# One scatter more per tile in the message pass, one less beside the first convolution

## The chip, the cores and the metric

One Trainium2 chip; the kernel runs on 1 of its cores. The metric is the device time in microseconds of one execution. The kernel before takes 4446.39 us, the median of three timed runs (4443.1 to 4448.91).

## The reference

A graph network of four layers on 6250 nodes with 96 features and 100000 edges that are sorted by destination. After each layer the result is added to x and normalised over the features.

```python
dst = (6250 * uniform(100000) ** 2).astype(int)       # then sorted; src is uniform
# layer 0: softmax aggregation
m = relu(x[src]) + 1e-7
a = exp(m - seg_max(m, dst)[dst]); a = a / seg_sum(a, dst)[dst]
x = norm(x + (x + seg_sum(a * m, dst)) @ W + b)
# layer 1: messages
msg = mlp(concat([x[src], x[dst], mlp(edge_attr)]))
x = norm(x + seg_sum(msg, dst) + mlp(x))
# layers 2 and 3: two mean convolutions each
conv(h) = (seg_sum(h[src], dst) / max(deg, 1)) @ Wl.T + b + h @ Wr.T
x = norm(x + conv(relu(conv(x)))); x = norm(x + conv(elu(conv(x))))
```

## The kernel before, in words

**Two edge passes.** The edges are padded and cut into 196 tiles of 512 (4 columns of 128 edges). The softmax pass and the message pass each go over the 196 tiles, with a ring of 4 tiles in the buffers. For each tile POOL issues four indirect DMAs that gather the source rows (L770, one for 128 edges). In the message pass SP loads two tiles at a time (L590 to L627): attributes, keys, flags, ranks, and eight windows of 128 rows of the destination table (L626, 48 KB each). PE sums the message in PSUM (L935, L941, L942; it waits for the gathers and windows), ACT applies relu and takes sums (L1230, L1234), DVE scans over the edges (L1682), PE turns the result back (L953), and ACT stores it.

**The adjacency matrix.** The four convolutions multiply with a matrix in DRAM, `adj`, of 51 x 51 blocks of 128 x 128 float16 counts. The softmax pass clears it. Each edge writes its count into one cell. During the message pass DVE computes for each tile the counts of its four columns (`count_copies`, L1643) and the cells (`redirect`, L1655). POOL writes them with indirect DMAs of 128 elements of two bytes, one for each column. The scatters in the pass go through the columns in order, NOW of them for each tile, three tiles behind: tile t issues columns NOW x (t - 3) and the next. So the first EARLY = 196 x NOW columns of the edge list are written in the pass, beside the gathers, in `gather_and_scatter` (L790, with the scatter at L781). Within it POOL takes the gathers in NOW portions and puts a scatter behind each; before the first scatter it waits for DVE's `redirected`. DVE's `redirect` waits until the scatters of the tile four before have landed.

**The late scatters.** The remaining columns, up to 782, are written by POOL after the pass (L855 to L862). Before them POOL gathers the ends of the runs for the node stage (L836, 49 of them). They go in batches of 8; after each batch POOL waits for the batch before it and raises `adj_ready` (L846 to L849).

**The first convolution.** PE first projects the nodes in 13 packs of four node tiles (L1072 transposes, L1083 matmuls, with DVE's `split_pack`, L1831, and ACT between). Then come 49 jobs, one for each node tile: 49 matmuls of 128 x 288 each (L1111) on a stripe of `adj`, 1568 KB, which SP loads into one of four slots (`fill_first`, L662). SP waits for `adj_ready` until the batches are in that hold the edges of the node tile; how many it needs is worked out on DVE from the degrees (`tile_ready`, L1522 to L1526). As the edges are sorted by destination, the job of node tile j needs all columns up to its last edge. Between and behind the jobs there are two joint jobs (L1120, of 49 matmuls; their stripes at L673, which wait for `ROWS_DONE` batches), then one load of 3136 KB of links (L680, once 48 jobs are summed), and the link matmuls (L1138) with the packs of the second convolution. The three other convolutions have 51 jobs each (L1181) and end the kernel.

Of the kernel before, what the change touches and what calls it, by code (L numbers as in the profile page):

```python
# [17 lines left out]
P = 128  # L18
F = 96
CH = 4  # L20
# [12 lines left out]
SLOTS = 4  # L33
PACK = 4
REPEAT = 1024
NOW = 2
BATCH = 8

MATRICES = ["W0", "W_node", "W_src", "W_dst", "W_ef"]
# [8 lines left out]
def joints(n_edges):  # L48

    return math.ceil(edge_tiles(n_edges) / P)  # L50
# [28 lines left out]
def build(nc, n_edges, x_in, chunk_last_in, node_rows_in, dst_cols_in, dst_before_in, dst_seq_in, src_cols_in, node_cols_in, next_row_in,  # L79
# [20 lines left out]
    EXT = joints(n_edges)  # L100
# [5 lines left out]
    SCATTERS = math.ceil(n_edges / P)  # L106
    EARLY = ET * NOW
    LATE = CN - EARLY
    BATCHES = math.ceil((SCATTERS - EARLY) / BATCH)
    assert LATE > 0 and SCATTERS > EARLY  # L110
    FIRST_ROUNDS = 7
    ROWS_DONE = [1 + math.ceil((min((i + 1) * P * CH, SCATTERS) - EARLY) / BATCH) for i in range(EXT)]
    assert ROWS_DONE[-1] == BATCHES + 1

    ctx = ExitStack()
    with ctx:
        def sb(name, shape, t=f32):
            return ctx.enter_context(nc.sbuf_tensor(name, shape, t))

        def dram(name, shape, t=f32):  # L120
            return nc.dram_tensor(name, shape, t, kind="Internal").ap()
# [18 lines left out]
        CELLS = JOBS * P * KB * P  # L140
        adj_all = dram("adj", [CELLS + (RING * NOW + LATE) * P, 1], f16)
        adj = adj_all[0:CELLS, :].rearrange("(t p c) a -> t p (c a)", p=P, c=KB * P)
# [125 lines left out]
        copies = tail(P, CN)  # L268
        cell_ring, is_repeat = sb("cell_ring", [P, RING, NOW], i32), sb("is_repeat", [P, RING, NOW], i32)
        copies_ring = sb("copies_ring", [P, RING, NOW], f16)  # L270
        elsewhere_late = cells(P, LATE).bitcast(i32)
# [7 lines left out]
        one_h = sb("one_h", [P, 1], f16)  # L279
        elsewhere = sb("elsewhere", [P, RING, NOW], i32)  # L280
        weigh = sb("weigh", [P, TE + (CH - 1) * P], bf16)
# [258 lines left out]
        def _(sp):  # L540
# [130 lines left out]
            def fill_joint(i):  # L671
                sp.wait_ge(adj_ready, ROWS_DONE[i])
                sp.dma_start(joint_slots[:, i, :, :].rearrange("p b n -> p (b n)"), adj[NT + i, :, 0:NT * P])\  # L673
                  .then_inc(joint_landed, 16)
# [33 lines left out]
        def _(pool):  # L708
# [3 lines left out]
            def iota(t, pattern, step):  # L712
                return nc.gpsimd.iota(t, pattern=pattern, base=0, channel_multiplier=step,
                                      allow_small_or_imprecise_dtypes=True)
# [30 lines left out]
            iota(iota_p[:, :], [[0, 1]], 1)  # L745
            nc.gpsimd.iota(elsewhere[:, :, :], pattern=[[P * NOW, RING], [P, NOW]], base=CELLS, channel_multiplier=1)
            nc.gpsimd.iota(joint_row[:, :], pattern=[[1, ET]], base=NP, channel_multiplier=0,
# [1246 lines left out]
```

How the kernel before makes its waits and increments, by code:

```python
def wait(eng, semaphore, value):  # L61
    if not (isinstance(value, int) and value <= 0):
        eng.wait_ge(semaphore, value)
# [8 lines left out]
    def do(self, instruction):  # L73
        self.n += 1
        instruction.then_inc(self.semaphore, 1)
        self.eng.wait_ge(self.semaphore, self.base + self.n)
# [446 lines left out]
        def wait_for_tables(eng, p):  # L523
            if PASSES[p] == MESSAGE:
                eng.wait_ge(node[p - 1]["stored"], 16 * NG)
                eng.wait_ge(node[p - 1]["dst_stored"], 16 * NT)
# [11 lines left out]
        @block.sync  # L539
        def _(sp):
            sp.dma_start(chunk_last, chunk_last_in).then_inc(lasts_landed, 16)
            sp.dma_start(attr_f, attr_in.rearrange("(p j) -> p j", p=P)).then_inc(attr_in_landed, 16)
            sp.dma_start(x_sb[:, 0:FULL, :], x_in[0:FULL * P, :].rearrange("(k p) f -> p k f", p=P)).then_inc(x_landed, 16)
            sp.wait_ge(consts_made, 1)
            sp.dma_start(x_sb[0:REST, FULL, :], x_in[FULL * P:n_nodes, :]).then_inc(x_landed, 16)
            sp.dma_start(w_edge[:, :], w_edge_in).then_inc(attr_in_landed, 16)
            sp.dma_start(seq_now, dst_seq_in[1:1 + EP].rearrange("(p j) -> p j", p=P)).then_inc(seq_landed, 16)
# [4 lines left out]
            sp.dma_start(src_cols, src_cols_in).then_inc(idx_landed, 16)  # L552
            sp.wait_ge(relu_made, 1)
            sp.dma_start(relu_table.rearrange("(k p) f -> p k f", p=P), hidden[:, 0:NT * F].rearrange(
# [72 lines left out]
                if kind == SOFT:
                    sp.wait_ge(zeros_made, 1)
                for h in range(RING // 2):
```

## Time and profile before

| | |
|---|---|
| Median of the timed runs | 4446.39 us |
| Span of the profiled execution, the only time that is given of it | 5171.8 us |
| PE busy | 3159.9 us (61%), 18737 matmuls |
| DVE busy | 2679.3 us (52%) |
| POOL busy | 2510.8 us (49%) |
| ACT busy | 1560.3 us (30%) |
| DMA | 387596 packets, 797.88 MB |
| Softmax pass, first to last gather | 84.2 to 1243.8 us |
| Message pass, first gather to last scatter | 1453.5 to 3186.7 us |
| Late scatters, first to last | 3268.4 to 3787.8 us |
| First link matmul | 4112.5 us |

All times in the rows are of that one profiled execution, counted from its first instruction. An engine's busy time leaves out register, branch and semaphore instructions and the issue of DMAs on SP and ACT; POOL's indirect DMAs are counted as busy. "issue" stands where an engine waited for nothing that the profile shows, "remote" where the release came from something that the profile doesn't name. SPq is SP's queue.

### The profile page before, as it was taken

Reading aid. Unit: us, or ns where it says so; the run is one execution under the profiler, and the core shown is the slowest. Engines: PE = TensorE matmul, PEld = TensorE weight load, DVE = VectorE, ACT = ScalarE, POOL = GpSimd, SP = SyncE. Lnnn points to the kernel's source line nnn. Section 1 sums busy time; section 2 is a strip of 40 time slices with the busy share of each in tenths; the row PEclk is TensorE's granted clock in tenths of the full one; section 3 lists DMA queues with packets and bytes.
Section 4 is the critical chain, followed back from the end, with each engine's and each line's share of the span. In section 5 each row is a group of like instructions: output and inputs, shape, how many; then the busy total and the mean of one; then the engine's idle time right before and its main releaser. Section 6 shows DMA issues by size and latency. Waiting matters only on the chain.

```text
span 5171.8 us, 61853 instructions
## 1 busy us (share of the span) xinstructions
PE 3159.9 (61%) x18737; PEld 2317.1 (45%) x18737; DVE 2679.3 (52%) x5868; ACT 1560.3 (30%) x3684; POOL 2510.8 (49%) x2587
## 2 busy tenths in 40 slices
PE   1555555554755555555555554111159999999999
PEld 0333333333534344344344333100047777788777
DVE  4888888888645555555555556300001254433333
ACT  1777777776222222222222222100000011111000
POOL 7666666664666666666666666777720000000000
PEclk9999999999986667667667666555579999999999
DMA  5555555555134444444444443100037666666776
GB/s 183 192 198 191 195 194 194 192 192 164 56 98 111 112 121 111 116 117 111 114 118 112 111 118 85 58 0 0 13 126 282 215 218 245 247 248 251 259 276 228
DMA packets 387596, 797.88 MB, mean 154 GB/s; under 512 B 207412, under 2 KB 264600, under 8 KB 361128
## 3 DMA queue, kind: packets, MB, share of 16 engines
q1 hardware_dynamic: 239330, 586.35, 33.9%
q0 software_dynamic: 82320, 90.28, 7.9%
q10 hardware_dynamic: 65718, 118.62, 6.2%
q8 instruction: 93, 1.52, 0.1%
q14 instruction: 135, 1.11, 0.1%
HBM read 581.03 MB, written 213.92 MB: 154 GB/s over the span
## 4 chain that ended last, share of the span: by engine, by line
PE 25%; issue 23%; SPq 19%; DVE 3%; another core or an unknown queue 1%; DMA 0%; ACTq 0%; ACT 0%; DVEq 0%; POOL 0%
PE ps L1181 18%; SPq L626 14%; PE ps L1111 6%; SPq L601 1%; SPq L596 1%; SPq L622 1%; SPq L607 1%; SPq L617 1%; PE ps L1064 1%; ACTq L64 0%; DMA area<-adj 0%; PE ps L1083 0%; PE ps L1056 0%; DVE second L1650 0%
## 5 line engine op out<-in xcount | busy, mean ns | idle before, releaser
L770 POOL DMA_INDIRECT area<-src_table,early x784 | 752.5, 960 | 469.6 <-remote 225.5
L770 POOL DMA_INDIRECT area<-relu_table,early x784 | 739.6, 943 | 421.3 <-issue 212.4
L953 PE MATMUL ps<-ident,area 96*128 96x96 f32 x2352 | 441.4, 356 | 804.3 <-issue 555.4
L953 PEld LDWEIGHTS ps<-ident,area 96*128 96x128 f32 x2352 | 355.2, 213 | 939.2 <-issue 782.4
L1181 PE MATMUL ps<-second,area 128*128 128x288 bf16 x5194 | 652.1, 286 | 0.2 <-DVE second L1823 0.2
L1682 DVE TENSOR_TENSOR_SCAN area<-flags,area,ps 96x512 f32<-96x512 int8 x196 | 250.0, 1276 | 647.6 <-issue 552.0
L1181 PEld LDWEIGHTS ps<-second,area 128*128 128x128 f16 x5194 | 509.0, 98 | 128.5 <-DVE second L1823 0.5
L1650 DVE SCALAR_TENSOR_TENSOR second<-second,area,ps 128x512 bf16<-128x512 f32 x784 | 538.1, 741 | 0.0
L857 POOL DMA_INDIRECT adj<-out_ring x390 | 395.5, 1014 | 127.8 <-issue 127.8
L781 POOL DMA_INDIRECT adj<-copies_ring,cell_ring x392 | 388.6, 991 | 125.6 <-issue 118.9
L1111 PE MATMUL ps<-early,area 128*128 128x288 bf16 x2401 | 322.0, 292 | 204.9 <-issue 204.9
L1230 ACT ACTIVATE ps<-ps,msg_bias 96x512 f32<-96x512 f32 x196 | 126.7, 647 | 1042.5 <-remote 911.0
L942 PE MATMUL ps<-second,area 128*96 128x128 f32 x1568 | 378.1, 328 | 34.1 <-issue 33.8
L941 PE MATMUL ps<-ident,area 128*96 128x128 f32 x1568 | 382.4, 334 | 7.8 <-issue 7.1
L941 PEld LDWEIGHTS ps<-ident,area 128*96 128x96 f32 x1568 | 301.0, 215 | 170.3 <-issue 170.2
L925 PE MATMUL ps<-ident,area 128*96 128x128 f32 x784 | 208.0, 421 | 265.8 <-DVE second L1705 184.9
L1111 PEld LDWEIGHTS ps<-early,area 128*128 128x128 f16 x2401 | 236.7, 99 | 290.0 <-issue 231.7
L916 PE MATMUL ps<-attr,w_edge_parts 36*96 36x512 bf16 x392 | 235.3, 601 | 185.2 <-DMA attr<-attr_parts 118.7
L1695 DVE TENSOR_TENSOR_SCAN second<-ps,second 96x512 f32<-96x512 f32 x196 | 249.5, 1273 | 159.7 <-remote 153.7
L1181 PE MATMUL ps<-early,area 128*128 128x288 bf16 x2597 | 331.8, 286 | 0.0
L935 PE MATMUL ps<-second,w_ef_scaled 96*96 96x512 f32 x392 | 306.6, 875 | 0.4 <-issue 0.4
L942 PEld LDWEIGHTS ps<-second,area 128*96 128x96 f32 x1568 | 283.8, 210 | 23.5 <-issue 23.4
(330 smaller groups left out, 4709.0 us busy)
## 6 DMA issues: line engine op xcount, KB each, us to landing
area<-adj SPq DMA_DIRECT2D x147, 1632.0 KB
area<-adj SPq DMA_DIRECT2D x55, 1568.0 KB
adj<-early SPq DMA_DIRECT2D x102, 816.0 KB
soft_sums<-out_ring ACTq DMA_DIRECT2D x196, 384.0 KB
second<-key_dram SPq DMA_DIRECT2D x98, 512.0 KB
area<-dst_table SPq DMA_DIRECT2D x784, 48.0 KB
sums<-out_ring ACTq DMA_DIRECT2D x196, 192.0 KB
second<-caps_dram SPq DMA_DIRECT2D x98, 192.0 KB
```

Source lines behind the costliest of these rows:

```text
L626: sp.dma_start(dst_rows[:, s + c // CH, c % CH, :], dst_table[bass.ds(firsts[c], P), :])\
L770: pool.indirect_dma_start(out=src_rows[:, s, c, :], out_offset=None, in_=gather_table[p], in_offset=bass.IndirectOffsetOnAxis(ap=src_cols[ ...
L781: pool.indirect_dma_start(out=adj_all, out_offset=bass.IndirectOffsetOnAxis(ap=cell_ring[:, s, c:c + 1], axis=0), in_=copies_ring[:, s, c: ...
L857: pool.indirect_dma_start(out=adj_all, out_offset=bass.IndirectOffsetOnAxis(ap=cell_late[:, c:c + 1], axis=0), in_=copies_late[:, c:c + 1] ...
L935: nc.tensor.matmul(bank(s % 2, F), w_ef_scaled[:, :], h_ring[:, s % 2, :], start=True, stop=False)
L941: nc.tensor.matmul(ps[0:F, s % 2, at], src_rows[:, s, c, :], ident[:, :], start=False, stop=False)
L942: last = nc.tensor.matmul(ps[0:F, s % 2, at], dst_rows[:, s, c, :], rank_hot[:, s % 2, at], start=False, stop=c == CH - 1)
L953: last = nc.tensor.transpose(ps[:, b, c * F:(c + 1) * F], r[:, (s * CH + c) * P:(s * CH + c + 1) * P], ident[0:F, 0:F])
L1111: last = nc.tensor.matmul(bank(lane % 2, P, PARTS_F), slots[:, lane, s, :], y[:, s, :, :].rearrange("p c f -> p (c f)"), start=s == 0, sto ...
L1181: last = nc.tensor.matmul(bank(b, P, PARTS_F), slots[:, lane, s, :], y[:, s, :, :].rearrange("p c f -> p (c f)"), start=s == 0, stop=s == ...
L1650: last = v.scalar_tensor_tensor(same[:, c, :], keys[:, s, :], key[:, bass.ds(t * CH + c, 1)].bitcast(f32), around, ALU.is_equal, ALU.mult, ...
L1682: v.tensor_tensor_scan(out=slot(sum_ring, s), data0=flags[:, s, :], data1=bank(s % 2, F), initial=last_of(sum_ring, s), op0=ALU.mult, op1= ...
```

## The change

NOW goes from 2 to 3: three scatters for each tile are issued in the message pass. EARLY, LATE, BATCHES, `tile_ready` and the rings that are NOW columns wide follow from it. With 588 early columns the first joint stripe (columns up to 512) needs no late batch, so the count for it is held at zero.

```diff
-NOW = 2
+NOW = 3
...
-    ROWS_DONE = [1 + math.ceil((min((i + 1) * P * CH, SCATTERS) - EARLY) / BATCH) for i in range(EXT)]
+    ROWS_DONE = [1 + math.ceil(max(min((i + 1) * P * CH, SCATTERS) - EARLY, 0) / BATCH) for i in range(EXT)]
```

In `gather_and_scatter` a tile's order on POOL changes from two gathers, scatter, two gathers, scatter to gather, scatter, gather, scatter, two gathers, scatter.

## Rows read from the trace of the kernel before

**Rows 1.** The page, part 4: the chain that ended last, by engine and line

```profile
PE 25%; issue 23%; SPq 19%; DVE 3%; another core or an unknown queue 1%; DMA 0%; ACTq 0%; ACT 0%; DVEq 0%; POOL 0%
PE ps L1181 18%; SPq L626 14%; PE ps L1111 6%; SPq L601 1%; SPq L596 1%; SPq L622 1%; SPq L607 1%; SPq L617 1%; PE ps L1064 1%; ACTq L64 0%; DMA area<-adj 0%; PE ps L1083 0%; PE ps L1056 0%; DVE second L1650 0%
```

**Rows 2.** Waits, 1900 to 3100 us: total us, times, longest us

```profile
POOL area L770 <- remote: 164.9, 62, 2.9
```

**Rows 3.** Timeline of POOL, two tiles: start us, us, [idle before]

```profile
2510.86 0.97 POOL L770 DMA_INDIRECT area<-src_table,early  x1 [2.52 <-remote]
...
2513.38 0.99 POOL L781 DMA_INDIRECT adj<-copies_ring,cell_ring  x1 [0.30 <-issue]
2514.68 0.96 POOL L770 DMA_INDIRECT area<-src_table,early  x1 [0.30 <-issue]
...
2528.39 0.97 POOL L770 DMA_INDIRECT area<-src_table,early  x1 [2.54 <-remote]
```

**Rows 4.** Windows: us, busy and count by engine, granted clock, DMA share, GB/s

```profile
1900.00:2500.00 600.00, 344.07 (x1566) 240.80 (x1567) 343.30 (x959) 168.10 (x409) 396.52 (x410) 0.69 0.44 115
```

**Rows 5.** Line L626, 1456.15 to 1458.2 us: ns min/median/max, first and last start

```profile
L626 SPq DMA_DIRECT2D area<-dst_table x4: 167/346/411, 1456.2 to 1457.8; - x4
```

**Rows 6.** Timeline of SP: the window loads of two tiles, later

```profile
2515.14 13.29 SPq L626 DMA_DIRECT2D area<-dst_table  x8
```

**Rows 7.** Timeline of PE: packs, then matmuls of early jobs

```profile
3283.72 1.47 PE L1083 MATMUL ps<-w_conv,hidden 97*128 97x192 f32 x8
...
3290.86 1.57 PE L1083 MATMUL ps<-w_conv,hidden 97*128 97x192 f32 x8 [1.99 <-issue]
...
3345.58 1.06 PE L1072 MATMUL ps<-ident,x_sb 128*96 128x128 f32 x4
...
3379.17 1.06 PE L1072 MATMUL ps<-ident,x_sb 128*96 128x128 f32 x4
...
3794.48 0.40 PE L1111 MATMUL ps<-early,area 128*128 128x288 bf16 x1 [2.40 <-issue]
3797.28 0.40 PE L1111 MATMUL ps<-early,area 128*128 128x288 bf16 x1 [2.40 <-issue]
...
3816.18 4.03 PE L1111 MATMUL ps<-early,area 128*128 128x288 bf16 x18 [0.28 <-issue]
```

**Rows 8.** Timeline of POOL: the late scatters, early and at their end

```profile
3283.03 0.97 POOL L857 DMA_INDIRECT adj<-out_ring  x1 [0.30 <-issue]
...
3787.76 1.09 POOL L857 DMA_INDIRECT adj<-out_ring  x1 [0.30 <-issue]
```

**Rows 9.** Lines L770, L781 and L857, whole trace, as in rows 5

```profile
L770 POOL DMA_INDIRECT area<-relu_table,early x784: 938/944/957, 84.2 to 1243.8; - x196
L770 POOL DMA_INDIRECT area<-src_table,early x784: 947/955/980, 1453.5 to 3171.7; - x196
L781 POOL DMA_INDIRECT adj<-copies_ring,cell_ring x392: 963/991/1005, 1471.1 to 3186.7; - x196
L857 POOL DMA_INDIRECT adj<-out_ring x390: 962/967/1907, 3268.4 to 3787.8; - x195
```

**Rows 10.** Timeline of DVE: the running maximum of two tiles

```profile
697.00 1.28 DVE L1695 TENSOR_TENSOR_SCAN second<-ps,second 96x512 f32<-96x512 f32 x1 [2.09 <-remote]
702.05 1.28 DVE L1695 TENSOR_TENSOR_SCAN second<-ps,second 96x512 f32<-96x512 f32 x1
```

**Rows 11.** DMA issues: KB each, median us to landing

```profile
second<-adj SPq DMA_DIRECT2D x2, 1568.0 KB, 9.7
area<-adj SPq DMA_DIRECT2D x1, 3136.0 KB, 14.1
```

**Rows 12.** Line L1138, as in rows 5

```profile
L1138 PE MATMUL ps<-early,area x294: 206/206/281, 4112.5 to 4153.9; 128*128 128x96 bf16 x147
```

**Rows 13.** Groups by line, 3820 to 4096 us: count | busy us, mean ns | idle

```profile
L1111 PE MATMUL ps<-early,area 128*128 128x288 bf16 x2206 | 270.6, 286 | 0.0
```

**Rows 14.** Groups by line, 1900 to 3100 us, DVE, as in rows 13

```profile
L1661 DVE TENSOR_SCALAR is_repeat<-area 128x2 int32<-128x2 f32 x136 | 26.0, 191 | 4.7
```

## The prediction

> **What bounds the kernel now.** I read the page's chain first [rows 1]. It names SP's window loads (L626) with 14% and gives 23% to "issue", time in which an engine waited for nothing that the profile shows. Taken as it stands, it says that SP paces the message pass. So I went to that pass. In the stretch from 1900 to 3100 us POOL waits 62 times for 2.7 us, once in two tiles [rows 2]. Its timeline shows the pattern [rows 3]: 12 indirect DMAs for two tiles, a gather every 1.26 us and a scatter every 1.30 us from start to start, then a pause; two tiles take 17.53 us, of which POOL needs 8 x 1.26 + 4 x 1.30 = 15.3 us, or 7.64 us a tile. PE and DVE are busy for 5.0 us a tile and ACT for 2.5 (POOL's count over its six a tile, 410 / 6 = 68 tiles in 600 us) [rows 4]. Only SP and POOL come near the pace.
>
> Then I asked whether SP's pace is real. At the start of the pass four window loads are issued 0.53 us apart [rows 5]; later eight of the same size take 13.29 us, 1.66 us each [rows 6]. PE shows the same in the first convolution: four-tile packs follow each other every 3.6 us at first (two in the 7.14 us shown) and every 33.6 us afterwards, and the matmuls of the first jobs stand 2.80 us apart, with no semaphore to blame [rows 7]. A pack is 12 matmuls and 12 weight loads, so 48 starts and ends: 0.70 us each. A job's matmul with its weight load has 4: 0.70 us again. POOL's late scatters go from 1.27 to 1.40 us at the end, each with its idle time before it, which is 2 x 0.70 [rows 8]. One start or end in 0.70 us, on three engines, whatever the work: I read this as the recording of the trace holding the engines, which a timed run doesn't have. That is an inference, and the sum tests it, since the span of 5171.8 us is 725 us above the median of 4446.39.
>
> **The time rebuilt without that.** First gather at 84 us [rows 9]. Softmax pass: 196 tiles at 5.05 us, the distance of two maxima without a wait [rows 10], 990. From its last gather (1243.8) to the message pass's first (1453.5), 210, taken as it is [rows 9]. Message pass: 196 x 7.64 = 1497. The tail, from the last scatter of the pass (3187.6) to the first link matmul: 81 until the late scatters start [rows 8, 9], 390 x 1.27 = 495, and since the last two node tiles need the last batch, one fill (9.7), one job and the links' load (14.1) behind it [rows 11]. A job is 6.0 us: 2206 matmuls in 270.6 us are 45 jobs [rows 13]. Together 606. From there to the end 5171.8 - 4112.5 = 1059 [rows 12]. Sum: 84 + 990 + 210 + 1497 + 606 + 1059 = 4446, the median itself. A sum that keeps SP's 8.77 us a tile would be 221 too long. So in the timed run POOL paces the message pass and, through the late scatters, the first convolution too.
>
> **The change, part by part.** EARLY goes from 392 to 588 columns. The pass gets 196 scatters more (one a tile), the late loop 196 fewer: 194 in 25 batches, for 390 in 49.
>
> Added to the pass: one scatter a tile on POOL. Bounds: nothing, if POOL had a wait of that size to fill (the trace's 2.5 us a pair [rows 3]; not below nothing, since an instruction more on POOL frees nothing earlier), and 1.40 us, the slowest pitch of any scatter [rows 8]. I take 1.30, the pitch in this very loop: 196 x 1.29 = 253 us, since POOL has no wait left in the rebuilt pass. The tile comes to 8.93 us on POOL. Queued behind the third scatter are the next tile's gathers; PE's score waits for these and everything else for PE. DVE's four small instructions handle three columns in place of two (0.19 us for the first of them [rows 14], and DVE is busy for 5.0 of 8.9 us): nothing; without that cover, under 0.1 us a tile. DVE's wait for its ring slot (four tiles back) is met one tile before POOL needs the cells. The DMA engines are 44% busy in the pass [rows 4]: room for 128 writes of two bytes more a tile.
>
> Removed from the tail: 196 x 1.27 = 249 us of POOL. All of it would count only if POOL stayed last. What is late next is PE. The four projected packs seen by 3292.4 are in native pace; nine more at 3.6 us end at 3325 [rows 7]; 48 jobs and the first joint at 6.0 us reach 3619, the links' load 3633 (the last job and second joint fit into it). The fills keep up: those 45 jobs have one 1568 KB fill each and no wait of PE [rows 13]. The scatters end at 3268 + 194 x 1.27 = 3515, about 100 us before PE gets to the last tile, and node tiles 0 to 26 now need none of them (the destinations are 6250 times a squared uniform number, so 75264 edges end at node 3540), so no batch holds a job. The first link matmul moves from 3187.6 + 606 = 3794 to 3633: a gain of 161 us, not 249. The other 88 us are scatters that were worth their time on POOL and now are not needed so early. Bounds of the gain: 0, if PE's jobs ran at the pace of POOL's batches for another reason, and 249. A small extra: before, PE idles between batches; in the pass a PE busy at 57% got a granted clock of 0.69, a mix of its two levels [rows 4], so the last three jobs may have run some 2.7 us slower than in my rebuild. I add 4 us to the gain, half of that.
>
> Sum: 4446 + 253 - 165 = 4534.
>
> A rule speaks against this. The Trainium skill, "NOTIFIC — the notification-queue block", section 10, says that emitting an implicit record costs the engine zero cycles; by it the 0.70 us steps would belong to the run, and the first rival below would hold. The same page, section 7.1, says that the block's internal pipeline holds back its producers rather than lose a record; by that the steps are the recorder's, and the forecast holds. The difference of 725 us between span and median agrees with the second.
>
> **The rivals.** (1) The pass is paced by SP as the trace has it. Then two more scatters (2.6 us) just about fill POOL's pause in a pair: 15.3 + 2.6 = 17.9 against 17.53, 0.2 us a tile, +35 us; and the tail still gains 161: 4446 + 35 - 161 = 4320, faster. For it: the chain, the pauses and that section 10. Against: the 0.53 us windows, and the sum that would be 221 too long. The change gains wherever POOL's idle time in a timed tile is over 0.47 us (253 - 161 = 92 us over 196). Chance 0.14. (2) POOL's instructions are cheaper in a timed run (1.2 us, say), and something else holds the tile at about 7.6. Then POOL has 0.4 us spare a tile: cost 196 x (1.2 - 0.4) = 157, gain 81 + 390 x 1.2 + 30 - 446 = 133: 4470, anywhere within 30 us of no change. For it: a recorder that slows others may slow POOL a little. Against: POOL's gathers take the same 0.94 to 0.98 us from 84 us on, before anything is held, to the end [rows 9]. Chance 0.10. (3) PE's slow stretch is real and ends with the scatters: 249 us earlier. With the 253 us of the pass that is 4450. For it: PE speeds up 25 us after the last scatter [rows 7, 8]. Against: the same sum. Chance 0.06. (4) The first convolution doesn't get shorter, because fills slow down beside scatters: 4446 + 253 = 4699. Against: PE didn't wait for one fill there [rows 13], and POOL's DMAs beside it are 128 times two bytes. Chance 0.06, with partial forms (jobs of 7 us, 4583) inside the forecast's range.
>
> **How the numbers follow.** The forecast has 0.64 and its own range of 4490 to 4590: POOL's pitch between 1.2 and 1.3 moves the difference to at most +100 (196 p in the pass, less 81 + 390 p + 30 - 446 in the tail, is 335 - 194 p), a job of 7 us adds 49. Faster: rival 1, and a third each of 2 and 3, 0.19. Same: 0.08, out of 2 and 3. Slower: 0.73, the forecast, rival 4 and the rest. Within 0.2% (9 us) is what a measurement of this kernel can't tell from no change. The range for 8 in 10 takes rivals 2 and 3 in: 4425 to 4600; it leaves out rival 1 and the full form of 4.
>
> **What would show it.** In the trace after: 588 scatters at L781 and 194 at L857; POOL's pauses in the pass gone or small, a tile at 8.9 us or more; the tail from the last scatter of the pass to the first link matmul shorter by at least 150 us; PE's stretch of 0.70 us steps shorter, since it goes with POOL's late scatters. Wrong, if the time falls although POOL has no pause, or if the pass's own length in the trace grows by less than 30 us and the time falls: then SP's pace was real.

## The result and the profile after

The changed kernel takes 4518.79 us (median of 4 runs, 4508.95 to 4521.51) against 4444.75 us for the kernel before beside it (4442.87 to 4448.91): a ratio of 1.0159, 95% interval 1.0147 to 1.0172 (the quotient of these two medians is 1.0167). The medians are 74 us apart, the changed kernel being slower. The forecast was 4534 in a range of 4425 to 4600, by 253 us more in the pass and 165 us less in the tail.

The trace of after isn't stretched as that of before was. Its span is 4507.2 us, and that execution was timed at 4508.95. So the rows of after can be set against the rebuilt times of the prediction, though not against [rows 9] directly. A trace of the unchanged kernel that can be set beside it is the first experiment.

The page of after, part 4, the chain that ended last:

```profile
POOL 29%; PE 28%; issue 10%; DVE 4%; DMA 1%; ACT 0%; DVEq 0%; SPq 0%; ACTq 0%; POOLq 0%
PE ps L1181 20%; POOL area L770 16%; POOL adj L781 13%; PE ps L1111 6%; PE ps L1064 1%; DMA area<-adj 0%; PE ps L1056 0%; PE ps L1083 0%; DVE out_ring L1839 0%; DVE out_ring L1837 0%; DVE second L1650 0%; DVE second L1775 0%; DVE second L1800 0%; DVE second L1768 0%; DVE second L1803 0%
```

In [rows 1] the window loads L626 had 14% and POOL 0%. Here L626 is gone from the chain; POOL's gathers and scatters have 29% between them. The late scatters (L857) are not in it at all, while the matmuls of the first convolution (L1111) are: POOL is last in the pass, PE in the tail.

Waits of POOL in after, 1900 to 3010 us (total us, times, longest us), and its timeline over one tile (start us, us, [idle before]):

```profile
POOL area L770 <- issue: 149.6, 491, 0.3
POOL adj L781 <- issue: 114.6, 376, 0.3
```

```profile
2512.35 0.99 POOL L781 DMA_INDIRECT adj<-copies_ring,cell_ring  x1 [0.30 <-issue]
2513.65 0.97 POOL L770 DMA_INDIRECT area<-src_table,early  x1 [0.30 <-issue]
2514.92 0.95 POOL L770 DMA_INDIRECT area<-src_table,early  x1 [0.30 <-issue]
2516.18 0.99 POOL L781 DMA_INDIRECT adj<-copies_ring,cell_ring  x1 [0.30 <-issue]
...
2520.04 0.97 POOL L770 DMA_INDIRECT area<-src_table,early  x1 [0.30 <-issue]
2521.32 0.99 POOL L781 DMA_INDIRECT adj<-copies_ring,cell_ring  x1 [0.30 <-issue]
```

The pause of 2.5 us in two tiles [rows 2, 3] is not there. POOL goes from one DMA to the next with 0.30 us between, and 867 such gaps in 1110 us are a start every 1.28 us. From scatter to the same scatter of the next tile (2512.35 to 2521.32) it is 8.97 us; the forecast was 8.93.

The lines of after that answer to [rows 9] and [rows 12] (ns min/median/max, first and last start):

```profile
L770 POOL DMA_INDIRECT area<-src_table,early x784: 947/968/980, 1256.2 to 2999.0; - x196
L781 POOL DMA_INDIRECT adj<-copies_ring,cell_ring x588: 963/991/1006, 1272.6 to 3011.8; - x196
L857 POOL DMA_INDIRECT adj<-out_ring x194: 962/967/1617, 3092.1 to 3347.6; - x194
L1138 PE MATMUL ps<-early,area x294: 206/206/281, 3449.6 to 3491.0; 128*128 128x96 bf16 x147
```

Windows of after (us, busy and count by engine, granted clock, DMA share, GB/s): the stretch of [rows 4], and the first convolution:

```profile
1900.00:2500.00 600.00, 369.05 (x1541) 271.37 (x1541) 337.96 (x937) 168.61 (x402) 457.21 (x469) 0.69 0.43 113
3140.00:3450.00 310.00, 307.60 (x2504) 245.06 (x2503) 44.80 (x119) 0.74 (x2) 154.84 (x160) 1.00 0.76 257
```

In the second one PE is busy for 307.6 of 310 us, at a granted clock of 1.00 (2.4 GHz). POOL's last late scatter starts at 3347.6, some 100 us before the first link matmul at 3449.6. PE paces the tail.

### The profile page after: what moved, and what is told of

The parts are those of the page before. It is cut to its first block, busy times and chain, and to the rows that moved or that the text cites. A ratio compares the mean times of both kernels' runs of the same rounds, so it can differ in the third digit from the quotient of the medians.

```text
span 4507.2 us, 61829 instructions
## 1 busy us (share of the span) xinstructions
PE 3202.6 (71%) x18737; PEld 2398.9 (53%) x18737; DVE 2674.5 (59%) x5868; ACT 1559.1 (35%) x3684; POOL 2505.2 (56%) x2587
## 4 chain that ended last, share of the span: by engine, by line
POOL 29%; PE 28%; issue 10%; DVE 4%; DMA 1%; ACT 0%; DVEq 0%; SPq 0%; ACTq 0%; POOLq 0%
PE ps L1181 20%; POOL area L770 16%; POOL adj L781 13%; PE ps L1111 6%; PE ps L1064 1%; DMA area<-adj 0%; PE ps L1056 0%; PE ps L1083 0%; DVE out_ring L1839 0%; DVE out_ring L1837 0%; DVE second L1650 0%; DVE second L1775 0%; DVE second L1800 0%; DVE second L1768 0%; DVE second L1803 0%
## 5 line engine op out<-in xcount | busy, mean ns | idle before, releaser
L941 PE MATMUL ps<-ident,area 128*96 128x128 f32 x1568 | 479.1, 405 | 664.8 <-DMA area<-src_table,early 664.3
L770 POOL DMA_INDIRECT area<-src_table,early x784 | 756.0, 964 | 240.6 <-issue 240.6
L770 POOL DMA_INDIRECT area<-relu_table,early x784 | 740.0, 944 | 239.0 <-issue 235.0
L941 PEld LDWEIGHTS ps<-ident,area 128*96 128x96 f32 x1568 | 341.5, 257 | 861.4 <-DMA area<-src_table,early 860.1
L781 POOL DMA_INDIRECT adj<-copies_ring,cell_ring x588 | 582.8, 991 | 179.2 <-issue 178.9
L953 PE MATMUL ps<-ident,area 96*128 96x96 f32 x2352 | 429.3, 349 | 133.9 <-ACT out_ring L1246 129.5
L942 PE MATMUL ps<-second,area 128*96 128x128 f32 x1568 | 454.8, 389 | 0.0
L925 PE MATMUL ps<-ident,area 128*96 128x128 f32 x784 | 210.5, 424 | 236.7 <-DMA area<-relu_table,early 149.7
L942 PEld LDWEIGHTS ps<-second,area 128*96 128x96 f32 x1568 | 355.0, 260 | 0.0
L1181 PE MATMUL ps<-early,area 128*128 128x288 bf16 x2597 | 331.7, 286 | 0.0
L1111 PE MATMUL ps<-early,area 128*128 128x288 bf16 x2401 | 295.9, 287 | 0.0
L1181 PEld LDWEIGHTS ps<-early,area 128*128 128x128 f16 x2597 | 253.8, 98 | 63.2
L925 PEld LDWEIGHTS ps<-ident,area 128*96 128x96 f32 x784 | 126.2, 189 | 295.4 <-DMA area<-relu_table,early 211.9
L1111 PEld LDWEIGHTS ps<-early,area 128*128 128x128 f16 x2401 | 235.6, 98 | 60.2 <-issue 0.2
L935 PE MATMUL ps<-second,w_ef_scaled 96*96 96x512 f32 x392 | 256.9, 742 | 0.4 <-ACT second L1278 0.4
```

What stands on the lines that cost most here:

```text
L770: pool.indirect_dma_start(out=src_rows[:, s, c, :], out_offset=None, in_=gather_table[p], in_offset=bass.IndirectOffsetOnAxis(ap=src_cols[ ...
L781: pool.indirect_dma_start(out=adj_all, out_offset=bass.IndirectOffsetOnAxis(ap=cell_ring[:, s, c:c + 1], axis=0), in_=copies_ring[:, s, c: ...
L925: last = nc.tensor.transpose(ps[0:F, s % 2, c * P:(c + 1) * P], src_rows[:, s, c, :], ident[:, :])
L935: nc.tensor.matmul(bank(s % 2, F), w_ef_scaled[:, :], h_ring[:, s % 2, :], start=True, stop=False)
L941: nc.tensor.matmul(ps[0:F, s % 2, at], src_rows[:, s, c, :], ident[:, :], start=False, stop=False)
L942: last = nc.tensor.matmul(ps[0:F, s % 2, at], dst_rows[:, s, c, :], rank_hot[:, s % 2, at], start=False, stop=c == CH - 1)
```

## The experiments

The first four ran beside runs of the kernel before that took 4437.51 us, the last three on another chip beside runs that took 4438.68, and the changed kernel itself beside 4444.75. So ratios are compared between these sets, not times.

### The kernel before with a fresh trace

No edit. It asks whether the 0.70 us steps, and with them SP's pace, belong to the kernel.

> The kernel before, unchanged, with a fresh trace. Theory A (the 0.70 us steps belonged to the recording of that one execution, and POOL paces the pass): a span of about 4443 us, a message-pass tile of 7.64 to 7.70 us in the trace (196 tiles, about 1503 us), POOL with no pause of 2.5 us in two tiles, and 606 to 617 us from the last scatter of the pass to the first link matmul. Theory B (the steps belong to the kernel's own work): a span near 5170 us again, with the window loads 1.66 us apart and POOL waiting 2.7 us in two tiles.

Measured: a span of 4445.3 us in a run timed at 4447.07. The lines, as above:

```profile
L770 POOL DMA_INDIRECT area<-src_table,early x784: 948/957/983, 1262.7 to 2755.6; - x196
L781 POOL DMA_INDIRECT adj<-copies_ring,cell_ring x392: 971/994/1008, 1280.3 to 2764.6; - x196
L857 POOL DMA_INDIRECT adj<-out_ring x390: 964/971/1657, 2847.4 to 3352.5; - x195
L1138 PE MATMUL ps<-early,area x294: 203/206/206, 3388.7 to 3429.1; 128*128 128x96 bf16 x147
```

Part 4 of its page, one group of SP's eight window loads, and POOL's waits from 1900 to 2760 us:

```profile
POOL 33%; PE 23%; issue 12%; DVE 3%; DMA 2%; ACT 0%; DVEq 0%; POOLq 0%
PE ps L1181 20%; POOL area L770 15%; POOL adj L857 8%; POOL adj L781 8%; POOL area L836 1%; DMA adj<-out_ring 1%; PE ps L1064 1%; DVE second L1650 1%; DMA area<-src_table,early 0%; DMA adj<-copies_ring,cell_ring 0%; PE ps L941 0%; PE ps L1056 0%; DMA area<-sums,end_row 0%; PE ps L942 0%; PE ps L1111 0%
```

```profile
2108.02 4.35 SPq L626 DMA_DIRECT2D area<-dst_table  x8
```

```profile
POOL area L770 <- issue: 136.5, 448, 0.3
POOL adj L781 <- issue: 67.4, 221, 0.3
POOL adj L781 <- DVE cell_ring L1666: 1.5, 5, 0.3
```

The same program gives a trace in which these steps are gone: eight window loads take 4.35 us where [rows 6] has 13.29, POOL has no wait over 0.3 us where [rows 2] has 2.9, and the span is 726 us shorter than that of the trace before. The steps belonged to that one recorded execution. Theory A holds, B falls. And POOL is last in the kernel before already, in the pass (L770 and L781 in the chain; 2765.6 - 1262.7 = 1503 us, 7.67 a tile) and in the tail (the late scatters, L857, have 8% of the chain, where after has none).

### The pass's half alone

```diff
-NOW = 2
+NOW = 3
...
-    EARLY = ET * NOW
+    EARLY = ET * 2
```

> The third scatter of each tile is added to the message pass, but the late loop still issues all its 390 (196 columns are written twice, with the same values). Theory A (POOL paces the pass, one scatter costs its full pitch, and nothing else in the pass changes): 4445 + 254 = 4699 us, between 4685 and 4710. Theory B (part of the third scatter hides in the pass, and the tail gained less than 180 us by the change): under 4640 us. Theory C (the extra wait of DVE or the longer ring costs beyond POOL): above 4720 us.

Measured: 4694.35 us, ratio 1.0576 (1.0559 to 1.0592), so +257 us, 1.31 for each of 196 scatters. The whole price of a scatter on POOL shows, with nothing hidden and nothing on top. In its trace the pass takes 1760 us (from 1262.3 to the end of the last scatter) and the tail 620:

```profile
L781 POOL DMA_INDIRECT adj<-copies_ring,cell_ring x588: 967/994/1008, 1278.7 to 3021.7; - x196
L1138 PE MATMUL ps<-early,area x294: 206/206/281, 3642.5 to 3683.9; 128*128 128x96 bf16 x147
```

### The tail's half alone

```diff
-    EARLY = ET * NOW
+    EARLY = ET * 3
```

with the same `max(..., 0)` as in the change. The 196 columns between are left out of `adj`; everything else is issued as in the kernel before.

> The pass keeps its two scatters a tile, the late loop has only the 194 of the change; the 196 columns between are left out of the adjacency. Theory A (the gain of the tail ends where PE becomes last, apart from the pass): 4445 - 180 = 4265 us, between 4250 and 4290, with 437 us from the last scatter of the pass to the first link matmul. Theory B (every late scatter was on the path, and PE is not last): 4445 - 249 = 4196 us. Theory C (the prediction's own size of the gain, 165 us, is right and the pass costs less than 253): 4280 us.

Measured: 4258.07 us, ratio 0.9593 (0.9578 to 0.9608), so -179 us. Not -249: of the 255 us that 196 scatters take on POOL (at 1.30), 76 are worth nothing. In its trace the pass is as before (1503 us) and the first link matmul comes 440 us after the pass's last scatter.

```profile
L781 POOL DMA_INDIRECT adj<-copies_ring,cell_ring x392: 971/994/1008, 1279.3 to 2763.5; - x196
L857 POOL DMA_INDIRECT adj<-out_ring x194: 964/971/1565, 2846.2 to 3103.0; - x194
L1138 PE MATMUL ps<-early,area x294: 206/206/281, 3204.5 to 3245.9; 128*128 128x96 bf16 x147
```

The two halves add up: 257 - 179 = 78 us, against 74 us for the change, 1.0169 against 1.0159 in ratios.

### The change in the other direction

```diff
-NOW = 2
+NOW = 1
```

> One scatter a tile in the pass and 586 in the late loop: the change in the other direction. Theory A (before, POOL is last in the pass and in the tail alike, so a scatter costs about the same in either place): 196 x 1.30 = 255 us less in the pass, 196 x 1.27 = 249 us more in the tail, so about 4440 us, between 4430 and 4455. Theory B (with five DMAs a tile something else than POOL paces the pass, at about 7.6 us a tile): up to 4694 us. Theory C (the pass gets faster down to five DMAs, 6.4 us, but PE or ACT holds a tile at 7.0 us): about 4560 us.

Measured: 4440.59 us, ratio 1.0004 (0.9995 to 1.0013). No difference. The pass is 261 us shorter, the tail 255 us longer:

```profile
L770 POOL DMA_INDIRECT area<-src_table,early x784: 947/952/981, 1258.6 to 2494.4; - x196
L781 POOL DMA_INDIRECT adj<-copies_ring,cell_ring x196: 967/991/1007, 1278.8 to 2499.5; - x196
L857 POOL DMA_INDIRECT adj<-out_ring x586: 962/967/1631, 2585.8 to 3341.4; - x196
L1138 PE MATMUL ps<-early,area x294: 206/206/287, 3379.0 to 3420.4; 128*128 128x96 bf16 x147
```

A tile is 6.34 us with five DMAs, 7.67 with six and 8.96 with seven: POOL's count sets it at each, and neither SP nor PE, DVE or ACT holds a tile above 6.34. So as long as POOL is last in both places, it doesn't matter where a scatter stands. The loss at three has to come from the tail, where POOL stops being last.

### Where POOL stops being last

The changed kernel, with some of the pass's scatters repeated by the late loop: 50 of them, and 120.

```diff
-    EARLY = ET * NOW
+    EARLY = ET * NOW - 50
```

> The changed kernel, whose late loop also repeats the last 50 scatters of the pass (same values; 244 in place of 194). Theory A (in the tail PE is last, and POOL's late scatters have a reserve): in the trace after, the last late scatter ends 101 us before the first link matmul; where POOL is last that distance is 35 us, so the reserve is 66 us or 51 scatters of 1.30. So 50 more cost 0 to 5 us: 1.016 to 1.017 times before, 4508 to 4514 us on this chip. Theory B (scatters beside the jobs slow PE's fills, so each costs its share): + 65 us, about 4575 us.

Measured: 4510.74 us, ratio 1.0162 (1.0147 to 1.0178); the change alone has 1.0159. 50 scatters, 65 us of POOL, cost nothing beyond the noise (each interval is some 6 to 7 us to either side). The tail in its trace is 438.7 us, from the end of the pass's last scatter (3011.1) to the first link matmul (3449.8), for 436.8 in after. PE's waits in its first convolution, 3138 to 3450 us:

```profile
PE ps L1138 <- DMA area<-adj: 2.0, 1, 2.0
PE ps L1111 <- DMA area<-adj: 1.4, 1, 1.4
```

The first signs of POOL being last again: a wait of 1.4 us for a fill, where after has none before L1111.

> The same with 120 scatters repeated (314 late). Theory A (POOL becomes last again beyond 51): (120 - 51) x 1.30 = 90 us above the changed kernel, about 4600 us, between 4590 and 4612; PE waits for fills again in the first convolution. Theory B (PE is last whatever POOL does): 4510 us. Theory C (every scatter costs): + 156 us, about 4665 us.

Measured: 4604.74 us, ratio 1.0378 (1.0362 to 1.0394): 94 us more than with 50. PE's waits from 3140 to 3546 us:

```profile
PE ps L1111 <- DMA area<-adj: 67.6, 15, 13.3
PE ps L1138 <- DMA area<-adj: 2.2, 1, 2.2
```

This fits free up to about 51 more, and the full 1.3 us each from there: (120 - 51) x 1.30 = 90. Between the two traces the tail grows by 89 us (438.7 to 527.8). So the bend lies near 194 + 51 = 245 late scatters; by the medians' 94 us it would be 242.

### Finer batches in the kernel before

```diff
-BATCH = 8
+BATCH = 4
```

> The kernel before with late batches of 4 scatters in place of 8. Theory A (the end of the tail hangs on the last batch, of 6 scatters in one and 2 in the other, and on 35 us of fill, job and load behind it): 0 to 6 us less than before, 4432 to 4438 us. Theory B (the semaphore waits of the finer batches cost POOL 49 more stops): up to 15 us more.

Measured: 4444.31 us, ratio 1.0014 (1.0005 to 1.0023): 6 us slower, so theory A falls and B's direction holds. POOL meets landings that are not yet in more often, 2830 to 3350 us in its trace:

```profile
POOL adj L857 <- DMA adj<-out_ring: 7.8, 13, 1.7
```

In the fresh trace of the kernel before that wait is 1.5 us, 5 times. The size fits, but its trace's span (4441.3, on another chip) is not longer than that of the fresh trace of before (4445.3), so the cause of the 6 us is not shown.

## Why the prediction was right, and where its sizes were off

**The pace of the pass: right.** The span of 5171.8 us was a stretched recording; the rebuilt time of 4446 was the kernel's (fresh trace: 4445.3). That it came out within 1 us was luck: up to the first gather of the pass the fresh trace has 1263 us where 1284 were rebuilt, in the pass 1503 for 1497, in the tail 623 for 606 and behind it 1057 for 1059, so an error of 21 us ahead of the pass covers the opposite ones behind it. Rivals 1 (SP paces, 4320) and 3 (PE's slow stretch is real) rested on rows that the fresh trace doesn't have. Rival 2 (cheaper instructions in a timed run, and 0.4 us spare a tile on POOL) is answered by timed runs: the pass's half alone costs 257 us, not 157. The sign that PE's stretch of 0.70 us steps would get shorter with the late scatters says nothing, since neither the fresh trace nor that of after has such a stretch.

What the steps were stays open. The prediction put them down to the recording; the spans of the eight later recordings lie within 1.8 us of their own runs' times, and no time is known of the first one's execution but its span. On the two sections of the Trainium skill, "NOTIFIC — the notification-queue block": the fresh trace is recorded too and has no step, which agrees with section 10 (a record costs the engine zero cycles); so that section didn't speak for rival 1. That producers can be held back (section 7.1) would fit the first trace, but no run here shows what held the engines in it.

**The added scatters: right.** 253 us forecast (196 x 1.29; with the 1.30 that the text names it is 255), 254 between the traces (1756.6 less 1502.9), 257 with the pass's half alone. Nothing of DVE's or SP's work became visible; DVE's waits for its ring slot (L1661) grew from 1.4 to 2.2 us each (76.8 us in 53 from 1900 to 2700, 131.9 us in 60 from 1900 to 2900) and stayed hidden.

**The tail: right in kind, 21 us too small in size.** POOL stops being last, and PE is next, as the prediction said. Rival 4 (no gain in the tail, 4699) falls with the tail's half alone, which gains 179 us, and PE waits for no fill before a job of after. From trace to trace the tail goes from 623 to 437 us, a gain of 186 where 165 were forecast. The terms:

- Before, 606 was forecast and 623 measured. The late loop took 506 us, not 495: 390 x 1.27 went by a single undisturbed row, and the mean pitch of the line is 1.30, as this row of the fresh trace has it (busy us, mean ns, idle):

```profile
L857 POOL DMA_INDIRECT adj<-out_ring x390 | 383.4, 983 | 125.3 <-issue 123.8 <-DMA adj<-out_ring 1.5
```

- Behind the last scatter 30 us were forecast (fill, job, links' load) and 35 measured, made up otherwise. The chain of waits of the fresh trace has 12.3 us from the last scatter's start to its landing, 7.2 of a fill, the last job at 8.6 in place of 6.0, and the second joint (L1120), which I took to be covered; the links' load is what hides there:

```profile
3352.46 12.32 DMA adj<-out_ring
3364.85 7.23 DMA area<-adj
...
3372.13 8.56 PE ps L1111 x49
3380.69 6.02 PE ps L1120 x49
```

The last job ran at a granted clock of 0.71, after PE had waited 8.9 us for its fill. The job before it had 0.68 after a wait of 4.7 us; both are mixes of the two levels, 1.2 and 2.4 GHz. The one before that, after a wait of 0.8 us, had 1.00 and 6.0 us for its 49 matmuls. This is the small extra of 4 us in the prediction; 2.5 us of it are on the path, since the other slow job is followed by a wait anyway. The last two jobs in PE's timeline, and windows of all three:

```profile
3354.36 8.91 PE L1111 MATMUL ps<-early,area 128*128 128x288 bf16 x49 [4.73 <-DMA area<-adj]
3372.13 8.56 PE L1111 MATMUL ps<-early,area 128*128 128x288 bf16 x49 [8.86 <-DMA area<-adj]
```

```profile
3343.50:3349.50 6.00, 6.00 (x49) 4.66 (x49) 0.04 (x1) 0.00 (x0) 4.74 (x5) 1.00 0.26 51
3354.40:3363.20 8.80, 8.80 (x49) 5.91 (x49) 0.00 (x0) 0.00 (x0) 0.00 (x0) 0.68 0.00 0
3372.10:3380.50 8.40, 8.37 (x49) 5.89 (x50) 0.00 (x0) 0.00 (x0) 0.00 (x0) 0.71 1.07 364
```

- After, 446 was forecast and 437 measured. The packs run ahead of the jobs every 2.9 us, not 3.6: that figure came from the two packs of [rows 7], in the stretched trace. Two packs of after, then the chain from the first job on:

```profile
3130.39 1.57 PE L1083 MATMUL ps<-w_conv,hidden 97*128 97x192 f32 x8 [0.86 <-ACT hidden L1388]
...
3133.26 1.57 PE L1083 MATMUL ps<-w_conv,hidden 97*128 97x192 f32 x8 [0.86 <-ACT hidden L1388]
```

```profile
3139.69 199.46 PE ps L1111 x1617
3339.16 6.00 PE ps L1120 x49
3345.16 90.05 PE ps L1111 x735
...
3435.22 14.33 DMA area<-adj
```

The jobs and the first joint take 295.5 us and the links' load 14.3, where 294 and 14 were forecast.

**The sum.** The traces differ by 254 - 186 - 6 = 62 us; the 6 are 4.9 us between the two passes and 1.6 in the softmax pass, less 1 behind the tail, for which I have no cause. The medians differ by 74, since the recorded execution of after was the fastest of its four, 9.8 us under their median, and that of the fresh trace 2.3 us over the median of before. A single trace can be 10 us off its kernel: the same fresh execution is 9.6 us over the median of the runs beside it. The forecast's 88 was too high, mostly by the tail.

**A shorter way to the number.** A scatter costs 1.29 to 1.33 us in the pass and 1.30 in the tail, so moving one is free while POOL is last in both. With PE last the tail is 437 us; POOL needs 82 + 1.30 x L + 35 for L late scatters, and that reaches 437 at L = 246, as the two experiments with repeated scatters bear out. The change goes from 390 to 194. The first 144 moved scatters cost nothing, and the other 52 cost 1.30 each: 68 us, between the 62 of the traces and the 74 of the medians. By the same line no share between pass and tail is faster than the kernel before (runs show it for one and for three scatters a tile only); a gain needs fewer instructions on POOL or use of its idle time. Some 60 us of that stand between the two passes (in the fresh trace POOL waits there 21.5 us for stores and 39.1 for ACT), but a scatter's copies are counted in the message pass, so filling it needs another order of the whole; that wasn't tried.

## What to carry to other kernels

When one engine issues the work on both sides of a move, moving it gains nothing while that engine is last on both; look for the point where that engine stops being last on one side, because from there each moved instruction costs its whole pitch on the other. Before trusting a profile that is longer than the timed run, rebuild the time from the rows that are not stretched, or record it again. For a term with hundreds of instructions use the mean of the line, idle time included: one clean row was 2% short, which was 11 us here.

## What the hardware showed beyond that

One recorded execution of the kernel before spanned 726 us more than another one of the same program (5171.8 and 4445.3), while the timed runs of it lie between 4431.4 and 4448.9. In the longer one starts and ends on PE stood 0.70 us apart, the last of POOL's late scatters 1.40, and register moves on SP (L626) that take 0.03 to 0.04 us in the second recording took up to 0.70. The profile put this down to "issue", to SP's queue and to "remote", and named SP's line as a main part of the chain; in the second recording that line is not among those that the chain names. POOL's gathers and scatters (L770, L781, L857) stand 1.25 to 1.33 us apart on average in every trace after the first, whether a row is a table's (L770) or a cell of two bytes, and whether the DMA engines are busy for 0.43 of the time or 0.76.
